# Second node stage of a four-layer graph network: three steps in one flow of seven chunks, with blocks taken two at a time in the halves of the array

## The chip, the cores and the metric

The kernel runs on one core of one Trainium2 chip. The metric is device time in microseconds (us); the time before is 21814.87 us, the median of three runs (21812.7 to 21848.82). The core has a matrix engine (TensorE, called PE in the profile, with its weight loads as PEld), three engines that work on rows of data (VectorE or DVE, ScalarE or ACT, GpSimd or POOL) and SyncE (SP), which issues DMAs here. Engines run side by side and wait for each other by semaphores. TensorE writes to PSUM, and VectorE and ScalarE copy from there to SBUF, from which DMAs go to memory. [...]

## The reference, cut to what matters

Four graph layers run one after the other on 12500 nodes with 64 features and 400000 edges. The stage that is changed closes the second layer and opens the third:

```python
Z = jax.ops.segment_sum(Y, id_Xe[1], num_segments=H.shape[0])      # acc: sums over edges
U_in = jnp.concatenate([H, Z], axis=1)
H_next = jax.nn.relu(U_in @ U_W.T + U_b)
...
x = x + _L1_gnn_ref(h, ...)                                        # x += H_next
h = jnp.maximum(_layernorm(x, axis=-1), 0.0)
# third layer: h @ weight[r] for each of 16 relations r; edges then gather rows of this table
msg = msg + h_src * mask[:, None].astype(feat.dtype) @ weight[r]
```

So for each of the nodes: an update from the old h and the sums, a layer norm, and a row of 16 x 64 = 1024 table values. All is float32.

## The kernel before, in words

The nodes stand in 98 blocks of 128 (`NB`), a block of rows on the 128 partitions, 64 features each. `CH` = 14 blocks make one of seven chunks (`CHUNKS`), `SUB` = 7 blocks one of fourteen half chunks (`SUBS`). The kernel is a row of stages with a barrier after each: building records, gather g0, message_table, gather g1, **update_table** (the stage changed), gather g2, and the last layer. Gather g2 reads the whole table that update_table writes, so nothing of it starts before.

update_table has two parts, one behind the other on TensorE. In the **first part** it takes each half chunk through `turn` (line 1011: h of 7 blocks is transposed by a product with the identity, 128 rows by 64 columns of the array, into `ps_t`), ScalarE copies the result to `ct` (line 971), and `product` (lines 1019 and 1020) adds two products for each block in `ps_u`: the sums `acc` with `uwa`, which takes all 128 rows of the array, and the turned h with `uwh`, which takes 64. VectorE adds bias and relu to x (lines 928 and 931) and runs the layer norm of a chunk (946, 949, 952, 959, 961), with ScalarE's square and square root (992, 998) between. There is one `ps_t`, so the next `turn` waits for ScalarE's copy. ScalarE's order is written out by hand: turned(2k+2), then the square of chunk k, which waits for line 952 of that chunk, then turned(2k+3), then the square root.

In the **second part** `turn_h` (line 1028) transposes the new h, ScalarE copies it (977), and `table_block` (line 1038) makes the 1024 values of a block in two products of 512 columns, with 64 of the array's rows. ScalarE copies the left half of each block (982) and VectorE the right half (936) from one of two `ps_m` to one of two `tb`, and SP writes the block (line 917, 512 KB). Each buffer comes free when its copies or its DMA are done.

A float32 product is two records in the trace, each a pass with a weight load of its own; "x14" for `turn` of 7 blocks is 14 passes.

Of the kernel before, what the change touches and what calls it, by code (L numbers as in the profile page):

```python
# [124 lines left out]
def build(nc, a, out):  # L125
    ctx = ExitStack()
    with ctx:
# [44 lines left out]
        update_table(nc, sem, a, Buffers(arena, b.at), psum, ident, epsc, x, acc, h, table)  # L172
# [711 lines left out]
def update_table(nc, sem, a, b, psum, ident, epsc, x, acc, h, dest):  # L884
# [9 lines left out]
    ct = [b.take(SUB * P) for _ in range(2)]  # L894
    pos = [b.take(SUB * D) for _ in range(2)]
    tb = [b.take(width) for _ in range(2)]
    assert b.at <= ARENA - NB * D
    names = ("w", "t", "ct", "u", "pos", "x", "total", "mid", "sq", "var", "std", "rs", "h", "th", "ht", "mm")
    s_w, s_t, s_ct, s_u, s_pos, s_x, s_total, s_mid, s_sq, s_var, s_std, s_rs, s_h, s_th, s_ht, s_mm = (sem("t2_" + n) for n in names)
    s_ca, s_cv, s_out = ([sem(f"t2_{n}{k}") for k in range(2)] for n in ("ca", "cv", "out"))  # L900
    ps_t = psum[:, 0:SUB * P]
    ps_u = [psum[:, 1024 + 512 * k:1024 + 512 * k + SUB * D] for k in range(2)]
    ps_m = [psum[:, 2048 + 1024 * k:3072 + 1024 * k] for k in range(2)]
    bias = ub.rearrange("p (o f) -> p o f", o=1).to_broadcast([P, SUB, D])

    with nc.Block() as block:
        @block.sync
        def _(sp):
            for k in range(2):
                sp.dma_start(uwa[k * D:(k + 1) * D, :], a["uw"][0:D, :]).then_inc(s_w, 16)  # L910
            sp.dma_start(uwh[0:D, :], a["uw"][D:2 * D, :]).then_inc(s_w, 16)
            sp.dma_start(ub, a["ub"].to_broadcast([P, D])).then_inc(s_w, 16)
            sp.dma_start(w[0:D, :], a["w2"]).then_inc(s_w, 16)
            for n in range(NB):
                sp.wait_ge(s_ca[n % 2], n // 2 + 1)
                sp.wait_ge(s_cv[n % 2], n // 2 + 1)
                sp.dma_start(dest[n * P:(n + 1) * P, :], tb[n % 2]).then_inc(s_out[n % 2], 16)
            for k in range(2):
                sp.wait_ge(s_out[k], 16 * (NB // 2))

        @block.vector
        def _(dve):
            v = nc.vector

            def update(s):
                dve.wait_ge(s_u, s + 1)
# [6 lines left out]
            def take_product(n):  # L933
                dve.wait_ge(s_mm, n + 1)
                wait_earlier(dve, s_out[n % 2], n // 2 * 16)
                v.tensor_copy(tb[n % 2][:, half:], ps_m[n % 2][:, half:]).then_inc(s_cv[n % 2], 1)

            dve.wait_ge(s_w, 80)
# [24 lines left out]
            for n in range(NB):  # L963
                take_product(n)

        @block.scalar
        def _(act):
            def turned(s):
                act.wait_ge(s_t, s + 1)
                wait_earlier(act, s_u, s - 1)  # L970
                nc.scalar.copy(ct[s % 2][0:D, :], ps_t[0:D, :]).then_inc(s_ct, 1)

            def turned_h(s):
                act.wait_ge(s_th, s + 1)

                wait_earlier(act, s_mm, (s - 1) * SUB)
                nc.scalar.copy(ct[s % 2][0:D, :], ps_t[0:D, :]).then_inc(s_ht, 1)

            def take_product(n):
                act.wait_ge(s_mm, n + 1)  # L980
                wait_earlier(act, s_out[n % 2], n // 2 * 16)
                nc.scalar.copy(tb[n % 2][:, 0:half], ps_m[n % 2][:, 0:half]).then_inc(s_ca[n % 2], 1)
# [3 lines left out]
            for k in range(CHUNKS + 1):  # L986
                if k + 1 < CHUNKS:
                    turned(2 * k + 2)
# [4 lines left out]
                if k + 1 < CHUNKS:  # L993
                    turned(2 * k + 3)
                if k >= 1:
# [3 lines left out]
            turned_h(0)  # L999
            for n in range(NB):  # L1000
                if n % SUB == SUB - 2 and n // SUB + 1 < SUBS:
                    turned_h(n // SUB + 1)
                take_product(n)

        @block.tensor
        def _(pe):
            def turn(s):
                wait_earlier(pe, s_ct, s)
                for j in range(SUB):
                    n = s * SUB + j  # L1010
                    last = nc.tensor.matmul(ps_t[0:D, j * P:(j + 1) * P], h[:, n * D:(n + 1) * D], ident, start=True, stop=True)
                last.then_inc(s_t, 1)

            def product(s):
# [761 lines left out]
```

## Time and profile before

| | us |
|---|---|
| median of three runs | 21814.87 |
| the profiled execution | 21835.44 |
| its span, first to last instruction | 21833.6 |
| TensorE busy in the span | 11628.7 (53%) |
| VectorE busy | 11929.5 (55%) |
| GpSimd busy | 15717.8 (72%) |
| mean granted TensorE clock, of 2.4 GHz | 0.667 |

A page of the profile gives each engine's busy time, a row of 40 slices of the span, DMA queues, and the costliest groups of instructions. The stage in question lies at 12403 to 12813 us, less than one slice of 546 us. So the page shows little of it, and what is read below comes from windows, groups by line and the order of instructions in that stretch.

### The profile page before, as it was taken

Reading aid. Unit: us, or ns where it says so; the run is one execution under the profiler, and the core shown is the slowest. Engines: PE = TensorE matmul, PEld = TensorE weight load, DVE = VectorE, ACT = ScalarE, POOL = GpSimd, SP = SyncE. Lnnn points to the kernel's source line nnn. Section 1 sums busy time; section 2 is a strip of 40 time slices with the busy share of each in tenths; the row PEclk is TensorE's granted clock in tenths of the full one; section 3 lists DMA queues with packets and bytes.
Section 4 is the critical chain, followed back from the end, with each engine's and each line's share of the span. In section 5 each row is a group of like instructions: output and inputs, shape, how many; then the busy total and the mean of one; then the engine's idle time right before and its main releaser. Section 6 shows DMA issues by size and latency. Waiting matters only on the chain. (4 is left out here: it accounts for less than half of the span.)

```text
span 21833.6 us, 187489 instructions
## 1 busy us (share of the span) xinstructions
PE 11628.7 (53%) x37787; PEld 5774.8 (26%) x37788; DVE 11929.5 (55%) x22486; ACT 4352.1 (20%) x10620; POOL 15717.8 (72%) x16724
## 2 busy tenths in 40 slices
PE   3777776455555556555555675555555222222246
PEld 1333333222222223222222332222222222222246
DVE  8777777655555555666666545555555222222246
ACT  3000000022222221111111110000000544444456
POOL 3777777777777775777777537777775777777776
PEclk7555555577777777777777777777776555555578
DMA  3333332222222221222222132222221333333366
GB/s 114 98 99 98 98 99 80 72 64 61 63 63 61 63 61 52 63 61 63 61 63 63 38 132 63 61 63 63 61 63 51 111 110 112 110 112 110 112 209 231
DMA packets 997084, 1873.16 MB, mean 86 GB/s; under 512 B 337172, under 2 KB 445620, under 8 KB 983812
## 3 DMA queue, kind: packets, MB, share of 16 engines
q1 hardware_dynamic: 481668, 1217.65, 17.3%
q0 software_dynamic: 506528, 652.41, 12.0%
q10 hardware_dynamic: 8800, 2.08, 0.0%
q8 instruction: 35, 0.57, 0.0%
q14 instruction: 53, 0.43, 0.0%
HBM read 1367.60 MB, written 503.37 MB: 86 GB/s over the span
## 5 line engine op out<-in xcount | busy, mean ns | idle before, releaser
L1289 PE MATMUL psum<-arena 128*128 128x512 f32 x9528 | 6683.6, 865 | 5301.0 <-DMA arena<-table,arena 1824.1
L1162 POOL DMA_INDIRECT arena<-table,arena x6352 | 6002.9, 945 | 2393.0 <-issue 1934.5
L1206 DVE TENSOR_TENSOR arena<-arena,psum 64x256 f32 x9528 | 3997.3, 420 | 4609.2 <-PE psum L1289 2610.5
L1289 PEld LDWEIGHTS psum<-arena 128*128 128x128 f32 x9528 | 2556.9, 283 | 9364.0 <-issue 7078.3
L712 POOL DMA_INDIRECT rec<-arena x3125 | 3003.9, 961 | 1270.4 <-issue 948.9
L1365 POOL DMA_INDIRECT rec<-arena x3176 | 3052.5, 961 | 1095.9 <-issue 962.7
L1162 POOL DMA_INDIRECT arena<-ptable,arena x3176 | 3001.2, 945 | 1115.9 <-issue 967.7
L1180 DVE TENSOR_TENSOR arena<-psum,arena 128x2048 f32<-128x2048 f32 x1191 | 2729.3, 2292 | 37.0
L1453 PE MATMUL psum<-arena 128*128 x6352 | 1086.9, 365 | 2937.4 <-DVE arena L1396 2747.9
L489 PE MATMUL psum<-arena 128*128 128x196 bf16 (+1 forms) x4375 | 1377.9, 428 | 1265.8 <-DVE arena L620 1265.8
L1386 DVE TENSOR_TENSOR arena<-arena 128x136 f32<-128x136 f32 x397 | 119.7, 301 | 2998.1 <-DMA arena<-rec 2997.9
L1453 PEld LDWEIGHTS psum<-arena 128*128 128x128 bf16 x6352 | 842.3, 133 | 3181.8 <-issue 3083.3
L1245 ACT ACTIVATE arena<-arena 128x64 f32<-128x64 f32 x3176 | 801.4, 335 | 3203.5 <-DMA arena<-table,arena 3203.5
L1418 ACT ACTIVATE arena<-arena 128x1024 bf16<-128x1024 bf16 x794 | 866.8, 1139 | 2156.2 <-DMA arena<-lanes 2156.2
L620 DVE TENSOR_TENSOR arena<-psum,arena 128x392 f32<-128x392 f32 x1875 | 918.1, 490 | 361.9 <-PE psum L489 236.6
L1239 ACT ACTIVATE arena<-arena 128x512 f32<-128x512 f32 x397 | 250.2, 630 | 3529.3 <-DVE arena L1186 3529.3
L489 PEld LDWEIGHTS psum<-arena 128*128 128x128 bf16 x4375 | 366.6, 115 | 2191.2 <-DVE arena L620 1815.8
L1423 ACT ACTIVATE arena<-arena 128x1024 bf16<-128x1024 bf16 x794 | 861.9, 1132 | 0.0
L1077 ACT ACTIVATE arena<-arena 128x98 f32<-128x98 f32 x1 | 0.4, 376 | 4060.9 <-DVE arena L734 4060.9
L581 ACT COPY arena<-arena 128x10 f32 (+1 forms) x625 | 127.2, 204 | 3178.1 <-DMA rec<-arena 3072.0
L625 DVE TENSOR_REDUCE arena<-arena 128x10 f32<-128x980 f32 x625 | 734.1, 1175 | 21.6
L1531 POOL TENSOR_SCALAR arena<-arena 128x128 bf16<-128x128 bf16 x880 | 636.5, 740 | 141.2 <-ACT arena L1543 140.1
(218 smaller groups left out, 10728.1 us busy)
## 6 DMA issues: line engine op xcount, KB each, us to landing
arena<-rec SPq DMA_DIRECT2D x297, 1408.0 KB
arena<-rec SPq DMA_DIRECT2D x440, 488.0 KB, 5.7
arena<-in_edge SPq DMA_DIRECT2D x625, 232.0 KB, 2.6
arena<-rec SPq DMA_DIRECT2D x400, 352.0 KB, 3.4
arena<-table,arena POOLq DMA_INDIRECT x6352, 2.5
arena<-lanes SPq DMA_DIRECT2D x99, 1024.0 KB
rec<-arena POOLq DMA_INDIRECT x6301, 2.3
table<-arena SPq DMA_DIRECT2D x196, 512.0 KB, 3.5
```

The lines of the kernel that those rows point to most:

```text
L489: return nc.tensor.matmul(to, identb, one_hots, start=False, stop=False, skip_group_check=True)
L620: v.tensor_tensor(prod[g][:, 2 * n * WIDE:2 * n * WIDE + w], run[:, 0:w], buf[g][:, 2 * n * WIDE:2 * n * WIDE + w], ALU.mult).then_inc(s_s ...
L712: nc.gpsimd.indirect_dma_start(rec, bass.IndirectOffsetOnAxis(ap=stage[g][:, j:j + 1], axis=0), recs[g][:, j * RW:(j + 1) * RW], None).the ...
L1162: nc.gpsimd.indirect_dma_start(rows[q][:, j * D:(j + 1) * D], None, tab, bass.IndirectOffsetOnAxis(ap=idx[:, j, field:field + 1], axis=0)) ...
L1180: v.tensor_tensor(hot[q % HB].rearrange("p (j w) -> p j w", w=LANES), iotas, fields(q, R_DSTL, 1).to_broadcast([P, G, LANES]), ALU.is_equa ...
L1206: v.tensor_tensor(block_sum, block_sum, ps[j // 2][half, j % 2 * LANES:(j % 2 + 1) * LANES], ALU.add).then_inc(s_add[j], 1)
L1245: last = nc.scalar.mul(rows[q][:, at], rows[q][:, at], fields(q, R_W, 1)[:, j, :])
L1289: last = nc.tensor.matmul(ps[u], rows[q][:, 2 * u * D:(2 * u + 2) * D], hot[q % HB][:, u * PAIR:(u + 1) * PAIR], start=True, stop=True)
L1365: nc.gpsimd.indirect_dma_start(slots, bass.IndirectOffsetOnAxis(ap=goal[q][:, j:j + 1], axis=0), rows[q][:, j * ROW:(j + 1) * ROW], None). ...
L1418: nc.scalar.activation(far[q % 2 * WIDEN + k], line, ACT.Square, bias=npid[k]).then_inc(s_far, 1)
L1423: nc.scalar.activation(hot_t[q % HB][:, k * G * P:(k + 1) * G * P], far[q % 2 * WIDEN + k], ACT.Relu, bias=ones[:, 0:1], scale=-1.0).then_ ...
L1453: last = nc.tensor.matmul(ps_m[q % 2][:, j * 256:j * 256 + HW], hot_t[q % HB][:, (k * G + j) * P:(k * G + j + 1) * P], hparts[:, bass.ds(a ...
```

## The change

Only `update_table` changes, and its call, which now also passes `shared`, a stretch of SBUF that this stage did not use.

- Both parts become one loop over k of `CHUNKS + 3` = 10 steps. In step k TensorE does: the updates of chunk k+1, the turning of old h for chunk k+2, the first 7 of 14 table units of chunk k-3 (`EARLY`), the turning of new h for chunk k-2, and the other 7 units. VectorE and ScalarE have their copies of table units spread between the steps of update and norm.
- Blocks are taken two at a time, block j of the first half chunk and block j of the second (`side` 0 and 1). Turning puts them on partitions 0 to 63 and 64 to 127 of one `ps_t`, so the copy of `ct` or `ht` is 128 x 896 for a whole chunk in place of two of 64 x 896. The products with `uwh` and with `w` use rows 0 to 63 of the array for one block and rows 64 to 127 for the other; `uwh` and `w` are loaded twice for that, one load for each half of the partitions.
- A table unit `u` is 512 columns of two blocks. ScalarE copies side 0 and VectorE side 1, so each makes 98 copies of 128 x 512, as before. There are still two sets of PSUM (`DUO` = 2), now of 1024 words as two banks, one for each side, and four `tb` of one block each, in place of two.
- In the updates the two products with `acc` come first and then the two with `ct`, in place of one of each by turns.
- `ct` and `ht` are now separate buffers, two of each.

```diff
-    ct = [b.take(SUB * P) for _ in range(2)]
+    ct, ht = ([b.take(SUB * P) for _ in range(2)] for _ in range(2))
...
-    tb = [b.take(width) for _ in range(2)]
...
+    extra = Buffers(shared)
+    tb = [extra.take(width) for _ in range(4)]
...
-    ps_m = [psum[:, 2048 + 1024 * k:3072 + 1024 * k] for k in range(2)]
+    DUO = 2
+    ps_m = [[psum[:, 2048 + 1024 * u + 512 * k:2048 + 1024 * u + 512 * (k + 1)] for k in range(2)] for u in range(DUO)]
+    PAIRS_K = NB // 2
+    EARLY = SUB
+    LAGS = CHUNKS + 3
     bias = ub.rearrange("p (o f) -> p o f", o=1).to_broadcast([P, SUB, D])
+    sides = [slice(k * D, (k + 1) * D) for k in range(2)]
...
             for k in range(2):
...
+                sp.dma_start(uwa[sides[k], :], a["uw"][0:D, :]).then_inc(s_w, 16)
+                sp.dma_start(uwh[sides[k], :], a["uw"][D:2 * D, :]).then_inc(s_w, 16)
+                sp.dma_start(w[sides[k], :], a["w2"]).then_inc(s_w, 16)
             sp.dma_start(ub, a["ub"].to_broadcast([P, D])).then_inc(s_w, 16)
...
+            for t in range(PAIRS_K):
+                for k, taken in ((0, s_ca), (1, s_cv)):
+                    n = t // SUB * CH + k * SUB + t % SUB
+                    sp.wait_ge(taken, 2 * t + 2)
+                    sp.dma_start(dest[n * P:(n + 1) * P, :], tb[t % 2 * 2 + k]).then_inc(s_out[t % 2 * 2 + k], 16)
+            for k in range(4):
+                sp.wait_ge(s_out[k], 16 * (-(-(PAIRS_K - k // 2) // 2)))
...
+            def take_products(k, units):
+                if not 0 <= k < CHUNKS:
+                    return
+                for u in range(k * CH + units[0], k * CH + units[1]):
+                    t, c = u // 2, u % 2 * half
+                    dve.wait_ge(s_mm[1], u + 1)
+                    if c == 0:
+                        wait_earlier(dve, s_out[t % 2 * 2 + 1], t // 2 * 16)
+                    v.tensor_copy(tb[t % 2 * 2 + 1][:, c:c + half], ps_m[u % DUO][1]).then_inc(s_cv, 1)
+            dve.wait_ge(s_w, 112)
             update(0)
             update(1)
-            for k in range(CHUNKS + 2):
+            for k in range(LAGS):
                 if k + 1 < CHUNKS:
                     update(2 * k + 2)
+                take_products(k - 3, (0, 2))
                 if k < CHUNKS:
                     dve.wait_ge(s_x, 2 * k + 2)
...
+                take_products(k - 3, (2, 4))
                 if 0 <= k - 1 < CHUNKS:
...
+                take_products(k - 3, (4, 6))
                 if k < CHUNKS:
...
+                take_products(k - 3, (6, EARLY))
                 if k + 1 < CHUNKS:
                     update(2 * k + 3)
-                if 0 <= k - 2:
+                if 0 <= k - 2 < CHUNKS:
...
+                take_products(k - 3, (EARLY, CH))
...
         @block.scalar
         def _(act):
...
+            def turned(k):
+                act.wait_ge(s_t, k + 1)
+                wait_earlier(act, s_u, k - 1)
+                nc.scalar.copy(ct[k % 2], ps_t).then_inc(s_ct, 1)
+            def turned_h(k):
+                act.wait_ge(s_th, k + 1)
+                for side in range(2):
+                    wait_earlier(act, s_mm[side], (k - 1) * CH)
+                nc.scalar.copy(ht[k % 2], ps_t).then_inc(s_ht, 1)
+            def take_products(k, units):
+                if not 0 <= k < CHUNKS:
+                    return
+                for u in range(k * CH + units[0], k * CH + units[1]):
+                    t, c = u // 2, u % 2 * half
+                    act.wait_ge(s_mm[0], u + 1)
+                    if c == 0:
+                        wait_earlier(act, s_out[t % 2 * 2], t // 2 * 16)
+                    nc.scalar.copy(tb[t % 2 * 2][:, c:c + half], ps_m[u % DUO][0]).then_inc(s_ca, 1)
             turned(0)
             turned(1)
...
+            for k in range(LAGS):
+                if k + 2 < CHUNKS:
+                    turned(k + 2)
+                take_products(k - 3, (0, EARLY - 1))
                 if k < CHUNKS:
...
+                take_products(k - 3, (EARLY - 1, EARLY))
+                if 0 <= k - 1 < CHUNKS:
...
+                if 0 <= k - 2 < CHUNKS:
+                    turned_h(k - 2)
+                take_products(k - 3, (EARLY, CH))
...
         @block.tensor
         def _(pe):
...
+            def turn(k, semaphore):
                 for j in range(SUB):
...
+                    for side in range(2):
+                        n = k * CH + side * SUB + j
+                        last = nc.tensor.matmul(ps_t[sides[side], j * P:(j + 1) * P], h[:, n * D:(n + 1) * D], ident, start=True, stop=True)
+                last.then_inc(semaphore, 1)
+            def turn_old(k):
+                wait_earlier(pe, s_ct, k)
+                wait_earlier(pe, s_ht, k - 4)
+                turn(k, s_t)
+            def turn_new(k):
+                pe.wait_ge(s_h, k + 1)
+                wait_earlier(pe, s_ht, k)
+                pe.wait_ge(s_ct, min(k + 5, CHUNKS))
+                turn(k, s_th)
+            def updates(k):
+                pe.wait_ge(s_ct, k + 1)
+                wait_earlier(pe, s_pos, 2 * k)
                 for j in range(SUB):
...
+                    to = [ps_u[side][:, j * D:(j + 1) * D] for side in range(2)]
+                    for side in range(2):
+                        n = k * CH + side * SUB + j
+                        nc.tensor.matmul(to[side], acc[:, n * P:(n + 1) * P], uwa, start=True, stop=False)
+                    for side in range(2):
+                        last = nc.tensor.matmul(to[side], ct[k % 2][sides[side], j * P:(j + 1) * P], uwh[sides[side], :], start=False, stop=True)
                 last.then_inc(s_u, 1)
...
+            def table_units(k, units):
+                if not 0 <= k < CHUNKS:
+                    return
+                for u in range(k * CH + units[0], k * CH + units[1]):
+                    j, c = u % CH // 2, u % 2 * half
+                    if u % CH == 0:
+                        pe.wait_ge(s_ht, k + 1)
+                    wait_earlier(pe, s_ca, u - DUO + 1)
+                    wait_earlier(pe, s_cv, u - DUO + 1)
+                    for side in range(2):
+                        nc.tensor.matmul(ps_m[u % DUO][side], ht[k % 2][sides[side], j * P:(j + 1) * P], w[sides[side], c:c + half],
+                                         start=True, stop=True).then_inc(s_mm[side], 1)
+            pe.wait_ge(s_w, 112)
+            turn_old(0)
+            turn_old(1)
+            updates(0)
+            for k in range(LAGS):
+                if k + 1 < CHUNKS:
+                    updates(k + 1)
+                if k + 2 < CHUNKS:
+                    turn_old(k + 2)
+                table_units(k - 3, (0, EARLY))
+                if 0 <= k - 2 < CHUNKS:
+                    turn_new(k - 2)
+                table_units(k - 3, (EARLY, CH))
```

## Rows read from the trace of the kernel before

**Rows 1.** Windows of the stage: start and end, length, busy of each engine, clock, DMA share, GB/s.
```profile
12410.00:12500.00 90.00, 76.65 (x308) 64.15 (x308) 13.19 (x18) 8.18 (x10) 0.00 (x0) 0.58 0.00 1
12500.00:12596.00 96.00, 72.12 (x279) 59.92 (x279) 23.81 (x32) 10.49 (x15) 0.00 (x0) 0.55 0.00 0
12606.00:12640.00 34.00, 34.00 (x73) 15.54 (x73) 8.58 (x12) 7.35 (x12) 0.00 (x0) 0.69 0.42 168
12640.00:12812.00 172.00, 170.17 (x503) 79.16 (x501) 60.13 (x87) 60.84 (x99) 0.00 (x0) 1.00 0.65 263
```

**Rows 2.** Groups by line: busy us, mean ns of one, idle before and releaser.
```profile
L1011 PE MATMUL psum<-arena 128*64 128x128 f32 x196 | 45.5, 425 | 42.6 <-ACT arena L971 30.8 <-DMA arena<-in_w 11.8
L1019 PE MATMUL psum<-arena 128*128 128x64 f32 x196 | 59.1, 398 | 6.1 <-ACT arena L971 6.1
L936 DVE COPY arena<-psum 128x512 f32<-128x512 f32 x98 | 67.7, 691 | 137.0 <-DMA table<-arena 74.4 <-PE psum L1038 62.5
L982 ACT COPY arena<-psum 128x512 f32<-128x512 f32 x98 | 57.4, 586 | 129.0 <-DMA table<-arena 79.1 <-PE psum L1038 49.8
L971 ACT COPY arena<-psum 64x896 f32<-64x896 f32 x14 | 12.5, 892 | 57.1 <-PE psum L1011 57.1
L928 DVE TENSOR_TENSOR arena<-psum,arena 128x448 f32<-128x448 f32 x14 | 8.7, 625 | 156.2 <-PE psum L1020 156.2
L961 DVE SCALAR_TENSOR_TENSOR arena<-arena 128x896 f32<-128x896 f32 x7 | 7.7, 1093 | 0.2
L959 DVE RECIPROCAL arena<-arena 128x14 f32<-128x14 f32 x7 | 1.6, 232 | 0.0
```

**Rows 3.** Timeline of TensorE, first part: start, length, instructions, idle before.
```profile
12410.31 3.25 PE L1011 MATMUL psum<-arena 128*64 128x128 f32 x14 [11.80 <-DMA arena<-in_w]
12414.54 3.25 PE L1011 MATMUL psum<-arena 128*64 128x128 f32 x14 [0.99 <-ACT arena L971]
...
12465.57 0.69 PE L1019 MATMUL psum<-arena 128*128 128x64 f32 x2
12466.19 0.61 PE L1020 MATMUL psum<-arena 64*128 64x64 f32 x2
12466.73 0.43 PE L1019 MATMUL psum<-arena 128*128 128x64 f32 x2
12467.09 0.43 PE L1020 MATMUL psum<-arena 64*128 64x64 f32 x2
...
12470.61 0.69 PE L1019 MATMUL psum<-arena 128*128 128x64 f32 x2
12478.05 1.33 PE L1011 MATMUL psum<-arena 128*64 128x128 f32 x5 [6.13 <-ACT arena L971]
```

**Rows 4.** Timeline of TensorE, second part.
```profile
12605.61 17.43 PE L1038 MATMUL psum<-arena 64*128 64x512 f32 x20 [5.87 <-ACT arena L977]
12622.97 3.25 PE L1028 MATMUL psum<-arena 128*64 128x128 f32 x14
12626.14 12.69 PE L1038 MATMUL psum<-arena 64*128 64x512 f32 x28
12638.77 1.74 PE L1028 MATMUL psum<-arena 128*64 128x128 f32 x14
```

**Rows 5.** Timeline, other stages: runs of passes of one shape at either clock.
```profile
16802.54 42.05 PE L1071 MATMUL psum<-arena 128*128 128x64 f32 x196 [3.34 <-PEq L110]
8378.46 3.25 PE L861 MATMUL psum<-arena 64*128 64x64 f32 x14
8384.57 1.77 PE L861 MATMUL psum<-arena 64*128 64x64 f32 x14
```

**Rows 6.** Line 917, the table's DMAs, and its row in the page's list of issues.
```profile
L917 SPq DMA_DIRECT2D table<-arena x98: 332/332/355, 12610.2 to 12811.7; - x98
table<-arena SPq DMA_DIRECT2D x196, 512.0 KB, 3.5
```

**Rows 7.** Windows of the loads that open gather g2, columns as in group 1.
```profile
12821.00:12823.00 2.00, 0.00 (x0) 0.00 (x0) 2.00 (x1) 0.00 (x0) 0.70 (x1) 0.50 1.04 400
```

**Rows 8.** Timeline of SP at the stage's start.
```profile
12403.86 1.12 SPq L910 DMA_DIRECT2D arena<-in_uw  x2
12406.29 0.47 SPq L913 DMA_DIRECT2D arena<-in_w  x1
```

More of the change, by code:

```diff
@@ L171, in build @@
         sem.end_stage()
-        update_table(nc, sem, a, Buffers(arena, b.at), psum, ident, epsc, x, acc, h, table)
+        update_table(nc, sem, a, Buffers(arena, b.at), psum, ident, epsc, x, acc, h, shared, table)
         sem.end_stage()
@@ L881, in _, with update_table @@
                 product(s)
-def update_table(nc, sem, a, b, psum, ident, epsc, x, acc, h, dest):
+def update_table(nc, sem, a, b, psum, ident, epsc, x, acc, h, shared, dest):
     width = R * D
@@ L925, in update @@
             def update(s):
-                dve.wait_ge(s_u, s + 1)
+                dve.wait_ge(s_u, s // 2 + 1)
                 wait_earlier(dve, s_x, s - 1)
@@ L998, in _ @@
                     nc.scalar.activation(rs[:, at], var[:, at], ACT.Sqrt, bias=epsc, scale=1.0 / D).then_inc(s_std, 1)
[L999 to L1003, printed above, removed]
+                if 0 <= k - 2 < CHUNKS:
+                    turned_h(k - 2)
+                take_products(k - 3, (EARLY, CH))
         @block.tensor
         def _(pe):
-            def turn(s):
-                wait_earlier(pe, s_ct, s)
+            def turn(k, semaphore):
@@ L1009, in turn @@
                 for j in range(SUB):
[L1010 to L1014, printed above, removed]
-                pe.wait_ge(s_ct, s + 1)
-                wait_earlier(pe, s_pos, s - 1)
-                for j in range(SUB):
-                    n = s * SUB + j
-                    nc.tensor.matmul(ps_u[s % 2][:, j * D:(j + 1) * D], acc[:, n * P:(n + 1) * P], uwa, start=True, stop=False)
-                    last = nc.tensor.matmul(ps_u[s % 2][:, j * D:(j + 1) * D], ct[s % 2][0:D, j * P:(j + 1) * P], uwh[0:D, :], start=False, stop=True)
-                last.then_inc(s_u, 1)
@@ L1023, in turn_h @@
-            def turn_h(s):
-                pe.wait_ge(s_h, s // 2 + 1)
-                wait_earlier(pe, s_ht, s)
-                for j in range(SUB):
-                    n = s * SUB + j
-                    last = nc.tensor.matmul(ps_t[0:D, j * P:(j + 1) * P], h[:, n * D:(n + 1) * D], ident, start=True, stop=True)
-                last.then_inc(s_th, 1)
-            def table_block(n):
-                s, j = n // SUB, n % SUB
-                if j == 0:
-                    pe.wait_ge(s_ht, s + 1)
-                wait_earlier(pe, s_ca[n % 2], n // 2)
-                wait_earlier(pe, s_cv[n % 2], n // 2)
-                for c in (0, half):
-                    last = nc.tensor.matmul(ps_m[n % 2][:, c:c + half], ct[s % 2][0:D, j * P:(j + 1) * P], w[0:D, c:c + half],
-                                            start=True, stop=True)
-                last.then_inc(s_mm, 1)
@@ L1042, in _ @@
-            pe.wait_ge(s_w, 80)
-            turn(0)
-            for s in range(SUBS):
-                if s + 1 < SUBS:
-                    turn(s + 1)
-                product(s)
-            pe.wait_ge(s_ct, SUBS)
-            turn_h(0)
-            for n in range(NB):
-                table_block(n)
-                if n % SUB == SUB - 3 and n // SUB + 1 < SUBS:
-                    turn_h(n // SUB + 1)
+                    for side in range(2):
+                        n = k * CH + side * SUB + j
+                        last = nc.tensor.matmul(ps_t[sides[side], j * P:(j + 1) * P], h[:, n * D:(n + 1) * D], ident, start=True, stop=True)
```

41 lines of the change are left out of this document (4 added, 37 removed).

## The prediction

> **What bounds the stage now.** The stage runs on its own between two barriers, so what it gains or loses is what the kernel gains or loses. I read the windows first [rows 1]: in the first part, 12410 to 12597 us, TensorE is busy 76.65 of 90 and 72.12 of 96 us, and no other engine is above a quarter. In the second, 12606 to 12812, it is busy 34 of 34 and 170.17 of 172 us. So TensorE's order sets the stage, and the question is at which clock its passes run and what makes it wait.
>
> The clock is read from the spacing of the passes. In the first part two passes take 0.62 us at 1.2 GHz (12465.57 to 12466.19) and 0.36 at 2.4 GHz (12466.73 to 12467.09), and the fast spell is short [rows 3]; the granted clock of 0.58 and 0.55 says the same [rows 1]. In the second part 28 passes of 512 columns take 12.69 us, mostly 0.43 each, once TensorE has worked without a gap for some 20 us; the 20 passes before took 17.43, most of them 0.86 [rows 4]. After that the clock is 1.00 throughout [rows 1].
>
> The waits: in the first part the turning idles 30.8 us and the product 6.1 us for the copy of line 971 [rows 2], mostly in gaps of 5 to 6 us a chunk (6.13 before 12478.05), and about 1 us where only the copy is late [rows 3]. The long gaps come from ScalarE's written order: turned(2k+3) stands behind the square, which waits for VectorE's line 952, which waits for products of TensorE. In the second part 524 KB at 263 GB/s are 1.99 us a block [rows 1], 0.25 of it the seventh part of a turning (1.74 [rows 4]), so **1.74 us** for the block itself. Lines 936 and 982 wait for DMAs 74 to 79 us and for TensorE 50 to 63 us [rows 2]: the two are about equally late there. The stage runs from the first pass at 12410.31 [rows 3] to the last table DMA at 12811.7 [rows 6]: **401.4 us**.
>
> **The change, part by part.** Prices are at 1.2 and 2.4 GHz.
>
> *Turning.* 14 passes take 3.25 or 1.74 us [rows 3, 4], so a chunk of 28 takes 6.5 or 3.5. Now consecutive products write to different halves of the array's columns. No row shows two such products; the bounds are no overlap (6.5 / 3.5) and full overlap (3.25 / 1.75). A turning pass loads 64 columns of weights and streams 128; a pass the other way round, 128 loaded and 64 streamed, takes 0.2145 us (42.05 / 196 [rows 5]), so the load of 64 needs no more than half of the 0.23. It is the streaming that two halves could share, and I take full overlap, and keep the other end.
>
> *Updates.* Passes of one shape in a row cost 0.2145 to 0.232 us at the lower clock and 0.126 at the higher [rows 5], but by turns between 128 rows and 64 rows of the array they cost 0.31 and 0.18 [rows 3]. So each change of shape costs about 0.17 / 0.12. A pair of blocks had 4 changes and 8 passes (2.48 / 1.45 us) and has 2 changes and 8 passes now: 8 x 0.22 + 2 x 0.17 = 2.1, or 8 x 0.122 + 2 x 0.12 = 1.22. Seven pairs: 15.1 / 8.5 us a chunk, before 17.4 / 10.2. Overlap of the two products with `ct` is not counted: the weight load of 128 columns is what spaces these passes.
>
> *Table.* A unit is two products, 4 passes: 1.71 / 0.86 us if the halves of the rows work at once, 3.42 / 1.72 if not. No row shows the overlap. The group's name says that each pass uses 64 of 128 rows [rows 4], and if the products start in order, the first pass of side 1 can still run beside the second of side 0. I take full overlap; the other end is a rival. A copy then becomes the limit: with two PSUM sets a set is refilled after 3 passes (1.29), a copy of 0.691 us [rows 2] and some 0.25 of handing over, so 2.24 for two units, **1.12 us** a unit at the higher clock, and (2.57 + 0.94) / 2 = **1.8** at the lower. The four `tb` add a DMA limit: a block's DMA lands 3.5 us after its issue [rows 6]; with 0.69 + 0.69 of copies behind it, two pairs of buffers turn in 5.6 us, 1.4 a unit once the first four of a run have used up the slack. The DMA engines allow more: 263 GB/s took a share of 0.65 [rows 1], loads ran at 400 GB/s [rows 7], so 524 KB need no less than 1.31 us. Seven units in a run: 4 x 1.12 + 3 x 1.5 = 9 us at the higher clock, 12.6 at the lower.
>
> [...]
>
> *Waits.* The gaps of 5 to 6 us go: ScalarE now copies `ct` before it waits for line 952. What is late next: about 1.1 us for the copy (0.99 in [rows 3]) four times in the opening, where nothing stands between a turning and its update. New is TensorE's wait for h in `turn_new`, in the middle of the units. Behind it stand units 7 to 13, and so both copiers and the DMAs. The wait is from the end of unit 6: copy 0.8, update 1.25 (twice line 928's 0.625), reciprocal 0.23, line 961's 1.09 [rows 2] and hand-overs, 3.7 us; from chunk 3 of the table on no update is left, 2.3. In the opening, turn_new(0) waits for a whole round of VectorE after updates(3), 7.4 us, of which turn_old(4) covers 3.25: 4.1.
>
> *Loads.* Two more DMAs on SP, 0.6 us each (1.12 for two [rows 8]): 1.2 us later at the start.
>
> *Clock.* The flow mixes stretches that had the lower clock (updates) with dense 512-column work that had the higher. I expect the lower clock in updates, as in the first part of before, and about half of each in the units and new turnings, as waits and updates come between them: the first seven units of a chunk near the lower price while updates stand before them, 10.5 to 11 else.
>
> **The sum**, at the lower clock for updates:
> - Opening, up to updates(4): 4 updates of 15.1, 6 turnings of 3.25, waits 3.3 + 4.1 = 87; the short fast spells of the first part take 7 off: 80.
> - Steps 3 and 4: 15.1 + 3.25 + 12.6 + 3.7 + 3.0 + 11, less 1 for a fast spell, = 48 each; step 5 has no old turning, 45: 141.
> - Steps 6 to 8: 10.5 + 2.3 + 2.5 + 10.5 = 26 each: 78. Step 9: 21.
> - Start 1.2 and end 1.
>
> Together 322, so 401 - 322 = **79 us less**. On the profiled execution of 21835.4 that gives 21756; that execution lies 20.6 above the median, to which the forecast applies: 21814.9 - 79 = **21736**. The forecast's own range: at the lower clock throughout 354 us (21768), without overlap of the turnings another 20 to 30 (up to 21790); with the higher clock in all units, 9 us for each seven, 288 (21702).
>
> **Rivals.**
> - *The higher clock holds throughout.* For: the second part held it for 170 us [rows 1]. [...] Opening 53, steps 3 to 5 99, 6 to 8 66, step 9 20, ends 2: 240 us, so 21654.
> - *The halves do not work at once.* Then the change does less than it says; a unit is 3.42 / 1.72 us. [...] TensorE is dense in the units, so the clock rises late in each early run: opening 100, steps 3 to 5 179, 6 to 8 90, step 9 24, ends 2 = 395 us, so 21809, no change.
> - *Slower: serial halves at the lower clock.* If besides the wait for h, every step, drops the clock to 1.2 GHz and updates hold it there, seven units cost 24 us. Opening 100, steps 3 and 4 80 each, step 5 73, steps 6 to 8 57 each, step 9 48, ends 2: 554 us, so 21967. It decides once the units run below 2.4 GHz for over about half their time without overlap, a stage of over 445 us. Against: such dense work brought the clock up within about 20 us before [rows 4].
>
> **Chances.** Forecast 0.60, higher clock 0.12, serial halves 0.22, slower 0.06. A difference of 0.2% (44 us) is about what a measurement of this kernel can tell from no change. Of the forecast's share a tenth lies within 44 us, of the serial case's a little on either side: faster 0.68, same 0.25, slower 0.07. The range leaves out the slower rival and half of the fastest: 21670 to 21820.
>
> **What would show it.** In the profile of after: the stage's length, 322 us from first pass to last table DMA. Start times of the table's passes: side 0 and side 1 side by side, a unit every 1.1 to 1.8 us; if the passes of a unit never overlap, the halves are serial. Turning of a chunk in 3.3 us at the lower clock against 6.5. Updates of a chunk near 15 us. TensorE's idle before the turning of new h, 2 to 4 us, released by line 961's successor. No gap of 5 us for `ct`. Spacing in the table's passes of 0.43 or 0.86 gives the clock. The prediction is wrong if the halves are serial, if the updates run at 2.4 GHz, or if DMAs of four buffers land later than 3.5 us so that units cost 1.75 us throughout.

## The result, and the profile after

| | us |
|---|---|
| before, median of 5 runs beside it | 21828.78 (21812.7 to 21848.82) |
| after, median of 5 runs | 21683.96 (21672.23 to 21689.39) |
| ratio | 0.9936, interval 0.9926 to 0.9947 |
| span of the profiled execution, before and after | 21833.6 and 21670.0 |
| the stage, first pass to last table DMA, before and after | 401.4 and 274.9 |

The kernel is 145 us faster. The forecast was 79 us, 21736; the range of 21670 to 21820 holds the time. Of the 145 us the stage gives 126. In the two profiled executions the stage also begins 15 us earlier, and what follows it is 22 us shorter, in stages that the change does not touch; I come back to that.

The windows of the stage after (columns as in [rows 1]) are the opening, steps 3, 4 and 5, and the rest:

```profile
12395.00:12465.00 70.00, 59.59 (x394) 51.88 (x395) 18.94 (x26) 7.99 (x11) 0.00 (x0) 0.60 0.00 1
12465.00:12505.00 40.00, 33.00 (x168) 20.87 (x167) 14.56 (x21) 11.00 (x18) 0.00 (x0) 0.72 0.34 138
12505.00:12540.00 35.00, 27.96 (x171) 16.77 (x169) 16.10 (x24) 11.12 (x20) 0.00 (x0) 0.85 0.53 214
12540.00:12573.00 33.00, 24.91 (x134) 14.47 (x136) 15.42 (x23) 9.56 (x16) 0.00 (x0) 0.79 0.50 202
12573.00:12671.00 98.00, 68.71 (x316) 30.34 (x315) 45.93 (x69) 37.77 (x64) 0.00 (x0) 0.93 0.78 316
```

TensorE is no longer busy throughout: 68.71 of the last 98 us. The clock is 0.60 in the opening and 0.93 in the last window, with 0.85 in step 4 and 0.79 in step 5 between. The lower and the higher clock, which the prediction calls 1.2 and 2.4 GHz, are granted clocks of 0.50 (12443.5 to 12446.2) and 1.00 (12573 to 12585); the windows give these shares and no frequency. The DMAs move 316 GB/s in the last window, against 263 in [rows 1]. That is a mean over units and turnings. In a run of units with no turning in it the DMA engines are full:

```profile
12573.00:12585.00 12.00, 8.91 (x36) 3.22 (x35) 8.47 (x13) 5.08 (x9) 0.00 (x0) 1.00 1.01 404
```

At 404 GB/s the 524 KB that a unit makes take 1.30 us, an estimate from this row.

The timeline of TensorE after shows each term of the sum (start, length, instructions, idle before). First the opening, then a chunk of units:

```profile
12395.21 3.25 PE L1031 MATMUL psum<-arena 128*64 128x128 f32 x28 [12.34 <-DMA arena<-in_ub]
...
12443.84 0.69 PE L1054 MATMUL psum<-arena 64*128 64x64 f32 x4
12444.46 1.11 PE L1052 MATMUL psum<-arena 128*128 128x64 f32 x4
12445.50 0.69 PE L1054 MATMUL psum<-arena 64*128 64x64 f32 x4
12446.13 1.11 PE L1052 MATMUL psum<-arena 128*128 128x64 f32 x4
...
12461.38 3.25 PE L1031 MATMUL psum<-arena 128*64 128x128 f32 x28 [4.10 <-DVE arena L978]
...
12492.48 3.26 PE L1031 MATMUL psum<-arena 128*64 128x128 f32 x28 [3.75 <-DVE arena L978]
...
12572.83 1.99 PE L1067 MATMUL psum<-arena 64*128 64x512 f32 x8 [1.56 <-DVE arena L949]
12575.39 1.99 PE L1067 MATMUL psum<-arena 64*128 64x512 f32 x8 [0.57 <-DVE arena L949]
12577.94 1.99 PE L1067 MATMUL psum<-arena 64*128 64x512 f32 x8 [0.57 <-DVE arena L949]
...
12586.98 3.11 PE L1031 MATMUL psum<-arena 128*64 128x128 f32 x28 [2.73 <-DVE arena L978]
```

Three things are to be seen. The halves work at once: 28 passes of turning take 3.25 us, as 14 did [rows 3], and 8 passes of 512 columns take 1.99 us, where one after the other at 0.43 each [rows 4] would need 3.4, an estimate. Two units come every 2.56 us, 1.28 each, about what the full DMA engines allow. TensorE waits 0.57 us of it for VectorE's copy (line 949), and the first copy of each such pair had itself waited for a DMA of the table (1.27 us before 12574.55 and before 12577.11). And the wait for the new h (line 978, the old 961) stands before each turning of new h.

### The profile page after: what moved, and what is told of

Read it like the earlier page. It is cut to its first block and busy times, and to the rows that moved or that the text cites. A ratio compares the mean times of both kernels' runs of the same rounds, so it can differ in the third digit from the quotient of the medians.

```text
span 21670.0 us, 187257 instructions
## 1 busy us (share of the span) xinstructions
PE 11478.3 (53%) x37787; PEld 5677.5 (26%) x37788; DVE 11916.9 (55%) x22486; ACT 4346.3 (20%) x10606; POOL 15688.8 (72%) x16724
## 5 line engine op out<-in xcount | busy, mean ns | idle before, releaser
L1318 PE MATMUL psum<-arena 128*128 128x512 f32 x9528 | 6680.8, 864 | 5287.7 <-DMA arena<-table,arena 1819.9
```

Source lines behind the costliest of these rows:

```text
L1318: last = nc.tensor.matmul(ps[u], rows[q][:, 2 * u * D:(2 * u + 2) * D], hot[q % HB][:, u * PAIR:(u + 1) * PAIR], start=True, stop=True)
```

## The experiments

On two of the chips used here every kernel, the one before too, takes 26.4 to 26.8 thousand us. The time is added in other stages: in the profile of after_again the products of line 1318 are preceded by 8308.1 us of idle, in that of after by 5287.7, with nearly the same busy time. The changed stage keeps its length there, 278.4 us for the kernel after against 274.9. So I compare stages, from the first pass to the issue of the last table DMA, and give medians against the kernel before on the same chip. The stage before was profiled on one chip only.

| kernel | stage, us | median less that of before, us |
|---|---|---|
| before | 401.4 | |
| order_only | 381.7 | -7 (one run) |
| flow_only | 360.5 | -45 |
| halves_only | 271.4 | -131 |
| after | 274.9 | -145 |
| after_again | 278.4 | -109 |
| h_first | 238.9 | -163 |
| h_first_eight | 222.3 | -171 (one run) |
| interleaved | 217.3 | -180 |
| ct_serial | 295.5 | -107 (one run) |
| turn_serial | 294.2 | -104 (one run) |
| table_serial | 423.0 | -8 (one run) |
| table_serial_again | 411.4 | +19 (one run) |

With eight buffers (h_first_eight and interleaved, below) more is still under way when the last DMA is issued: the next stage issues its first DMA 4.6 us later in after and h_first, 7.3 in h_first_eight and 7.1 in interleaved.

### Halves without the flow, and the flow without halves

**halves_only** puts the table behind the last update, with blocks still in pairs:

```diff
-    LAGS = CHUNKS + 3
+    LAGS = CHUNKS + 9
...
-                table_units(k - 3, (0, EARLY))
-                if 0 <= k - 2 < CHUNKS:
-                    turn_new(k - 2)
-                table_units(k - 3, (EARLY, CH))
+                table_units(k - 9, (0, EARLY))
+                if 0 <= k - 8 < CHUNKS:
+                    turn_new(k - 8)
+                table_units(k - 9, (EARLY, CH))
```

with the same shift for ScalarE's and VectorE's copies and for turned_h. The turning of new h now waits until all of `ct` is copied.

> The blocks still go two at a time in the halves of the array, but the table waits for the last update: two parts one behind the other, as before. Stage after the change: 275 us from first pass to last table DMA. Theory A (the halves are the gain, the one flow brings nothing, since TensorE works through its order one by one either way and the flow adds a wait for the new h in each chunk): updates and turnings 7 x (11.7 + 3.3) + 8 of waits = 113, gap for h 8, table 7 x (1.75 + 14 x 1.28) = 138, together about 258 us, so at or below the kernel after the change, ratio to before about 0.993. Rival B (the flow brings a third or more of the gain, by keeping TensorE busy while copies and DMAs run): 310 us or more, ratio 0.996.

Measured: stage 271.4 us, ratio 0.9951 (0.9935 to 0.9968). It has ScalarE's new order too (see order_only). Theory A holds: **the flow adds nothing to the halves**. The table's part of its timeline:

```profile
15814.89 7.84 PE L1066 MATMUL psum<-arena 64*128 64x512 f32 x24 [10.05 <-ACT arena L994]
15824.31 1.13 PE L1066 MATMUL psum<-arena 64*128 64x512 f32 x4 [1.59 <-DVE arena L949]
15825.37 1.75 PE L1031 MATMUL psum<-arena 128*64 128x128 f32 x28
15827.05 5.18 PE L1066 MATMUL psum<-arena 64*128 64x512 f32 x20
```

There is one gap of 10.05 us between the parts, and then no wait for h in front of any turning: it takes 1.75 us at a granted clock of 1.00 (15825.4 to 15827.1) right behind a unit. What the flow saves at the seam and in the updates (75.2 us of products against 83.8 here) it pays back in seven waits for h, 25.0 us.

**flow_only** keeps the flow and lets both blocks use the same rows or columns (it does not compute the values of the side 1 blocks):

```diff
-   matmul(ps_t[sides[side], ...
+   matmul(ps_t[sides[0], ...
-   ct[k % 2][sides[side], ...], uwh[sides[side], :]
+   ct[k % 2][sides[0], ...], uwh[sides[0], :]
-   ht[k % 2][sides[side], ...], w[sides[side], c:c + half]
+   ht[k % 2][sides[0], ...], w[sides[0], c:c + half]
```

> One flow as after the change, but all products of side 1 use the same rows or columns of the array as side 0, so no two can run at once (the values of the side 1 blocks are wrong for it; the work in instructions and bytes is the same). Theory A (the halves are the whole gain): turnings 14 x 3.2 = 45 us more, the products with the turned h 7 x 4 = 28, table units 1.8 to 2 in place of 1.3 at the higher clock and twice at the lower, 50 to 60: stage 395 us or more, ratio to before about 1.000. Rival B (the flow alone gives a third or more): stage 350 us or less, ratio 0.998.

Measured: stage 360.5 us, ratio 0.9983 (0.9973 to 0.9993). This lies between the two expectations: everything but the halves brings 41 us. That is not the flow by itself, since the kernel also has ScalarE's new order, the grouping of the updates' products by shape, and four `tb`. The updates' products sum to 92.2 us here (45.3 and 46.9), against 118.0 in the kernel before (59.1 in [rows 2] and 58.9 in the row below), and ScalarE's order is worth 20 us in the next experiment. No run has the flow without these, so a gain of its own is not shown.

```profile
L1020 PE MATMUL psum<-arena 64*128 64x64 f32 x196 | 58.9, 395 | 0.0
```

The group of its table passes, and that of after (the second row):

```profile
L1067 PE MATMUL psum<-arena 64*128 64x512 f32 x392 | 182.5, 625 | 0.0
```
```profile
L1067 PE MATMUL psum<-arena 64*128 64x512 f32 x392 | 104.1, 645 | 28.5 <-DVE arena L949 23.0 <-ACT arena L1004 4.8
```

The same 392 passes keep TensorE for 182.5 us instead of 104.1, and it waits for no copy.

### ScalarE's order alone

**order_only** is the kernel before with one line of ScalarE's order moved:

```diff
                 if k + 1 < CHUNKS:
                     turned(2 * k + 2)
+                    turned(2 * k + 3)
                 if k < CHUNKS:
...
-                if k + 1 < CHUNKS:
-                    turned(2 * k + 3)
```

> The kernel before with one line moved: ScalarE copies turned(2k+3) before the square of chunk k and not after it. Theory A (the long gaps of TensorE in the first part came from ScalarE's order): the gaps of 5 to 6 us a chunk go, 37 us of idle fall to about 10, and with TensorE dense the clock may rise: stage 401 less 25 to 45, 355 to 375 us, which is the whole of what the flow without the halves gains (41 us). Rival B (the gaps come from the single ps_t buffer, and what is moved changes nothing): 395 us or more.

Measured: 381.7 us, 20 less than before. The size falls short of theory A's 25 to 45, and the timeline shows that the gaps went all the same. The turning's group and the second part:

```profile
L1010 PE MATMUL psum<-arena 128*64 128x128 f32 x196 | 44.9, 421 | 12.0 <-DMA arena<-in_w 11.0 <-ACT arena L971 1.0
```
```profile
15685.82 17.43 PE L1037 MATMUL psum<-arena 64*128 64x512 f32 x20 [6.09 <-ACT arena L977]
...
15762.34 7.13 PE L1037 MATMUL psum<-arena 64*128 64x512 f32 x16
15770.78 9.86 PE L1037 MATMUL psum<-arena 64*128 64x512 f32 x12 [1.30 <-DVE arena L936]
15780.57 3.25 PE L1027 MATMUL psum<-arena 128*64 128x128 f32 x14
```

The idle for ScalarE's copy falls from 36.9 us [rows 2] to 1.0, and the first part from 195.3 us (12410.31 to 12605.61, [rows 3, 4]) to 154.2: **41 us**, 36 of it gaps and most of the rest updates at a slightly higher clock (granted 0.61 in the first part, 0.57 before). Then the second part takes 227.5 us against 206.1: behind one wait of 1.30 us, from 15769.5 on, passes go from 0.43 to 0.82 us and the turning from 1.74 to 3.25 (granted clock 0.51 from 15771 to 15809, 1.00 before). With that the second part takes 21 us back. So in the first part this one line, which needs no flow, brings as much as flow_only in all, and 20 us are left of it in this one run. All kernels with the new code have it.

### Each pair of halves alone

**ct_serial**, **turn_serial** and **table_serial** make one of the three edits of flow_only each.

> Only the products of the turned old h (64 of 128 rows) use rows 0 to 63 for both blocks (x of the side 1 blocks is wrong for it). In the profile of after the four passes of a pair take 0.62 us at the lower clock and 0.37 at the higher. The prediction held that the weight load spaces these passes, so that the halves give nothing here (Theory A: stage within 3 us of the 275 to 278 after). Rival B: weight loads in the two halves of the rows overlap too, and without the halves the four passes take 1.0 us and 0.55: 49 x 0.3 = 15 to 20 us longer.

Measured: 295.5 us, 17 to 21 more than after: rival B. The group of the turned products without the halves and, second, in after:

```profile
L1054 PE MATMUL psum<-arena 64*128 64x64 f32 x196 | 47.4, 384 | 0.0
```
```profile
L1054 PE MATMUL psum<-arena 64*128 64x64 f32 x196 | 29.6, 393 | 0.0
```

The timeline of a pair of blocks at the lower clock (granted 0.50 from 12442 to 12445):

```profile
12442.09 1.11 PE L1052 MATMUL psum<-arena 128*128 128x64 f32 x4
12443.14 1.11 PE L1054 MATMUL psum<-arena 64*128 64x64 f32 x4
12444.18 1.11 PE L1052 MATMUL psum<-arena 128*128 128x64 f32 x4
```

Without the halves the four passes of line 1054 take 1.04 us from start to start, with them 0.62 (12443.84 to 12444.46 above). The loads of line 1054 take 0.27 us each in both kernels, and together they cover 38.9 us in ct_serial and 21.2 in after. So the weight loads in the two halves of the rows run beside each other too.

> Only the turning writes to PSUM partitions 0 to 63 for both blocks (the blocks of side 1 are wrong for it). Theory A (consecutive turnings in different halves of the columns overlap fully): a turning of 28 passes goes from 3.25 to 6.5 us at the lower clock and from 1.75 to 3.4 at the higher; 14 of them with about a third at the higher clock, 35 to 40 us longer, about 312 us, unless TensorE's longer activity raises the clock and gives 10 to 20 back. Rival B (only the rows matter): within 5 us of 275 to 278.

Measured: 294.2 us, 16 to 19 more. The turnings keep TensorE 72.6 us against 42.7, 30 more, near theory A's 35 to 40. 11 to 14 came back: the waits for h are 20.6 us against 25.0, the table's passes sum to 101.4 us against 104.1, and the updates' products to 70.7 against 75.2, at a slightly higher clock (granted 0.81 over the stage against 0.79).

> Only the table's products of side 1 use rows 0 to 63, like side 0 (the table rows of the side 1 blocks are wrong for it). Theory A (the halves work at once, and the copies bound a unit at 1.28 us): a unit takes 4 x 0.43 = 1.72 us and some 0.1 at the higher clock, so 98 x 0.5 = 50 us longer at least, stage 325 to 345 us. Rival B (the halves hardly overlap, the gain is from elsewhere): stage below 290 us.

Measured: **423.0 us**, 150 more than after and 22 more than before. Neither theory: the overlap is real, but its loss costs three times the 50 us expected, since 252 of the 392 passes took 0.86 us, the spacing at a granted clock of 0.50 (15918 to 15966), and 140 took 0.44 or 0.45. Here are runs of both kinds in table_serial, and below flow_only, which has more serial work:

```profile
15765.22 24.26 PE L1067 MATMUL psum<-arena 64*128 64x512 f32 x28
...
15804.26 12.65 PE L1067 MATMUL psum<-arena 64*128 64x512 f32 x28
...
15889.70 24.61 PE L1067 MATMUL psum<-arena 64*128 64x512 f32 x56
15918.35 48.15 PE L1067 MATMUL psum<-arena 64*128 64x512 f32 x56
15971.74 24.55 PE L1067 MATMUL psum<-arena 64*128 64x512 f32 x56
16000.38 72.05 PE L1067 MATMUL psum<-arena 64*128 64x512 f32 x84
```
```profile
15830.58 12.28 PE L1067 MATMUL psum<-arena 64*128 64x512 f32 x28
15936.26 24.30 PE L1067 MATMUL psum<-arena 64*128 64x512 f32 x56
16029.53 36.31 PE L1067 MATMUL psum<-arena 64*128 64x512 f32 x84
```

For the last 84 passes in a row a pass takes 0.86 us in the one (granted clock 0.50) and 0.43 in the other (1.00). In flow_only only 28 of the 392 passes, at 15903.18, took 0.86.

> The kernel of table_serial once more: its stage took 423 us, with the units of 28 passes at 24.3 us (lower clock), while flow_only, with more serial work, took 360 us with 12.3 us (higher clock). Theory A (which clock the units get depends on the order of waits and dense work, so on the kernel): 24 us for the first units and 415 to 430 us again. Rival B (it is a matter of the moment at which the run begins, and falls otherwise each time): the stage comes out elsewhere between 330 and 430 us.

Measured on another chip: 411.4 us. The last runs alternate as before (24.52, 48.15, 24.46 and 72.05 us); of the early ones two of 28 passes took 12.4, where one did, so 224 passes ran at the lower clock, 0.86 us each. That speaks for theory A, that most of the lower clock belongs to that kernel, though the length just misses the window expected for it. What in the kernel decides it stays open.

### Where the wait for h goes, and what is late next

**h_first** moves the block that makes h(k-2) on VectorE (wait for s_std, reciprocal, scalar_tensor_tensor) ahead of `update(2 * k + 2)`, with nothing else changed.

> The reciprocal and the scaling that make the new h of chunk k-2 are moved to the head of VectorE's step, before the updates and copies. After the change TensorE waits 38 us before the turning of new h and loads, 25 of them for the step that makes h (2.6 to 5.1 us each). Theory A: nothing else is late there, all seven waits go and the stage gets 20 to 25 us shorter, about 252 us. Rival B: the copies of the units, moved back by 1.3 us, or the DMAs of the table come to be late next, and the gain is below 10 us.

Measured: 238.9 us, ratio 0.9945 (0.9928 to 0.9962); 36 to 40 less than after and after_again. All seven waits are gone; the group of the turning in h_first:

```profile
L1031 PE MATMUL psum<-arena 128*64 128x128 f32 x392 | 35.8, 356 | 13.5 <-DMA arena<-in_ub 11.4 <-ACT arena L987 2.1
```

and after:

```profile
L1031 PE MATMUL psum<-arena 128*64 128x128 f32 x392 | 42.7, 405 | 38.3 <-DVE arena L978 25.0 <-DMA arena<-in_ub 12.3 <-ACT arena L987 1.0
```

25.0 us of waiting went, and with it another 11 to 15, of which 7 are turnings at a higher clock (35.8 against 42.7 us for the same passes) and 4 to 5 are updates (70.7 against 75.2). The granted clock over the stage is 0.84, and 0.79 in after.

**h_first_eight** has eight `tb` besides, four pairs in turn (`tb[t % 4 * 2 + k]`).

> h_first with eight tb in place of four. Theory A (copies bound the units, the waits of VectorE for DMAs of the table, 45 us in h_first, are mostly hidden by TensorE's wait for copies): 0 to 8 us less than 239. Rival B (the DMAs of four buffers bound the units): 20 us less or more, 1.15 us a unit.

Measured: 222.3 us, 17 less: nearer to B. Up to the next stage's first DMA it is 14 less (229.6 against 243.6). VectorE's waits for the table's DMAs fall from 44.9 to 16.9 us (h_first, then h_first_eight):

```profile
L949 DVE COPY arena<-psum 128x512 f32<-128x512 f32 x98 | 64.3, 688 | 65.5 <-DMA table<-arena 44.9 <-PE psum L1067 20.6
```
```profile
L949 DVE COPY arena<-psum 128x512 f32<-128x512 f32 x98 | 65.8, 688 | 42.8 <-PE psum L1067 26.0 <-DMA table<-arena 16.9
```

So in after the four buffers, and with them the landing of DMAs, held back the copies that TensorE seemed to wait for. With eight, nine units in a row take 1.02 us each, with no wait shown:

```profile
15688.83 9.21 PE L1067 MATMUL psum<-arena 64*128 64x512 f32 x36
```

The DMAs now go on through turnings and updates, and the engines stay full over whole steps. The first window is h_first_eight, the second interleaved, which comes next:

```profile
15680.00:15720.00 40.00, 36.46 (x188) 14.14 (x186) 28.82 (x42) 22.14 (x39) 0.00 (x0) 1.00 1.02 405
15660.00:15700.00 40.00, 37.72 (x192) 14.05 (x190) 25.97 (x39) 21.47 (x38) 0.00 (x0) 1.00 1.02 405
```

**interleaved** goes further: eight `tb`, h one step earlier, and on TensorE a piece of other work behind each unit:

```diff
+            NEW = {0: (0, 2), 1: (2, 4), 2: (4, 6), 3: (6, 7)}
+            OLD = {11: (0, 3), 12: (3, 5), 13: (5, 7)}
+            for k in range(LAGS):
+                for i in range(CH):
+                    table_units(k - 4, (i, i + 1))
+                    if i in NEW:
+                        turn_new(k - 3, NEW[i])
+                    elif i in OLD:
+                        turn_old(k + 2, OLD[i])
+                    else:
+                        updates(k + 1, (i - 4, i - 3))
```

> The flow of the changed kernel, but each unit of the table is followed by one piece of an update or of a turning (an update of one pair of blocks takes 0.96 us at the higher clock), the new h is made a step earlier, and there are eight tb. Theory A (TensorE stands idle in each unit for the copy, some 0.57 us in 2.57 for two units, and the copiers and DMAs stand idle during updates, so only interleaving makes the one flow pay): opening four steps of 15 = 60, seven steps of 14 x 1.45 = 142, together 205 us. Rival B (TensorE's order is the bound, pieces and units add up as before): 235 us or more, no better than h_first at 239.

Measured: 217.3 us, ratio 0.9926 (0.9908 to 0.9944), median 26409.21 us (26394.19 to 26410.96) beside 26480.3 us (26471.89 to 26490.99) for the kernel after on the same chip (after_again). It beats both kernels, by 71 us over after. But only 5 us of that is the interleaving, since h_first_eight has 222.3. Theory A's 205 was not reached, and the theory had no term for the DMA engines: 98 blocks of 524 KB at 405 GB/s are 127 us, an estimate from the windows above, and the first is issued 82.5 us after the first pass. Together that is 209 us to the landing of the last, and some 5 less to its issue. So 205 would have needed full engines from the first DMA on, and what is left to gain in such a kernel lies mostly in the opening.

> The kernel after the change itself, beside the others of this call, as the reference for stage lengths on the same chip. The stage had 275 us from first pass to last table DMA. If a stage length is a property of the kernel, it is 270 to 280 again; if the clock falls otherwise from run to run, it can be off by 20 us or more, and the comparisons of single profiles are worth no more than that.

Measured: 278.4 us, as expected. A stage length repeats within some 4 us for this kernel and within 12 for table_serial, by two profiles each; so the 5 us of interleaved over h_first_eight, and the 3 to 7 of halves_only under after, are not told from zero by single profiles.

## Why the prediction was right, and where it was off

The forecast was right in direction and in its main mechanism, the overlap of the halves, and short by 66 us in size, 47 of them in the stage: 322 predicted, 274.9 measured. That is nearer to the 240 of its first rival, the higher clock throughout. Two terms are off. The updates are seven chunks at 15.1, 106 us, less some 10 for fast spells, and their products took 75.2 (45.6 and 29.6); without the overlap they took 93.9 (ct_serial, 46.5 and 47.4), so nearly all of this error is the overlap that was not counted. The units add up to 155 us in the sum, and the table's passes with the waits for copies took 132.6 (104.1 and 28.5), since the clock was above the "about half of each" of the text.

- **Opening**, 80 predicted, 69.4 measured (12395.21 to 12464.56). The term for updates failed: "Overlap of the two products with `ct` is not counted: the weight load of 128 columns is what spaces these passes." A chunk takes 7 x 1.67 = 11.7 us at the lower clock, not 15.1, and ct_serial shows why. The price of grouping by shape was right: without the overlap a pair takes 2.09 us there, as summed (2.1). The wait for the first h was 4.10 (4.1 predicted); the others in the opening were 1.00 for ScalarE's copy and 5.1 for VectorE, where the sum had 3.3.
- **Turnings**: full overlap, 3.25 us for 28 passes, as taken. That a load of 64 columns needs no more than half of the 0.23, the reason given for it, is not shown: in the kernel before, the records of the loads last 0.226 us in line 1011 (64 columns) and 0.269 in line 1019 (128).
- **Steps 3 and 4**, 48 predicted each, 40.7 and 34.7 measured (12464.56 to 12505.25 to 12539.92). In step 3 the updates give 3.4 us, the units, quicker than the price at the lower clock, most of the rest. In step 4 most of the updates ran at the higher clock, a pair in 0.96 us (granted clock 1.00 from 12505 to 12508); "the lower clock in updates" was wrong for most of steps 4 and 5. The prediction named updates at the higher clock as a sign that it is wrong, and for these two chunks that sign came.
- **Units**: 1.12 us if copies bound them, 1.5 when DMAs do; measured about 1.04 for the first five of a run (5.18 us for 20 passes) and 1.28 after. Once no updates are left seven take 9.1 to 10.3 us, near the 9 us of the price at the higher clock (the sum has 10.5), but by two errors that cancel: copies allow 1.02 (h_first_eight), and the DMAs bind at 1.28, by the full engines. The prediction had that bound, "no less than 1.31 us", and set it aside for one from the landing time. Of that one the terms named, 3.5 and twice 0.69, make 4.9 us and not 5.6, and 3.5 is a median over the 196 DMAs of two stages [rows 6]. The 0.25 us of handing over in the price of 1.12 is shown by no run; 1.02 leaves 0.06 for it (2.04 for two units less 1.29 and 0.69), an estimate.
- **Wait for h**: 3.7 predicted beside updates and 2.3 after them; measured 3.75, 3.94 and 5.13, then 2.73, 2.64 and 2.71. Right in place and nearly in size. But its price is not its length alone: without it the stage is 36 us shorter, not 25, in part by the clock.
- **Step 5 to the end**, 144 predicted, 130 measured (12539.92 to 12670.1), from the updates of step 5 and the clock: the last window stands at 0.93, above the half and half of the sum.
- **The gaps of 5 to 6 us** came from ScalarE's order, as the text had it: order_only leaves 1.0 of 36.9 us [rows 2]. What is late next in the changed kernel is ScalarE's copy once (1.00 us; the text says four times 1.1, its sum has three) and, once the updates follow each other, VectorE's bias add that frees `ps_u`, 5.1 us in all in the opening. The two more DMAs cost less than the 1.2 us predicted: the idle before the first pass is 12.34 us against 11.80 [rows 3], and it lies ahead of the stage as measured here.
- **Outside the stage**: 19 us of the 145 are not in it. Where the same comparison was made on other chips, medians and stages moved alike (halves_only -131 and -130, h_first -163 and -162.5, flow_only -45 and -41) or the median less (after_again -109 and -123). In the single runs the two differ by up to 30 us (order_only -7 and -20, table_serial -8 and +22, table_serial_again +19 and +10). So 19 us are within what differs without a known cause, and they are not shown to be an effect of the change.

Of the rivals, serial halves did not happen (8 passes of 512 columns in 1.99 us), but the slower one was closer than its chance of 0.06 says. Once only the table's products are made serial in this flow, 252 and 224 of the 392 passes take 0.86 us, the lower clock, and the stage is longer than before (423.0 and 411.4 us). Its threshold was put at 445 us, the 401.4 of before and 44 more; the two runs stay under that. The reason I gave against it, that dense work brings the clock up within some 20 us [rows 4], did not hold there.

The copies by themselves are only a small part of TensorE's wait here. With eight buffers a unit takes 1.02 us, against 0.86 for its four passes of 0.43, two at a time; the rest of the wait is the DMAs'.

## What to carry to other kernels

Pairing products that use half of the array's rows or columns paid here in float32, and for short passes too (four of 64 columns in 0.62 us instead of 1.04). With ScalarE's order, products grouped by shape and four buffers it gave 130 us of a stage of 401, and the one flow gave nothing beside it. Before overlapping stages on an engine that works in written order, ask what it waits for in the middle: moving the step that it waits for ahead of others (h_first) gave 36 us for seven moved lines, more than the flow. When copies look like the limit, see what they wait for, and look at the DMA share in a window of such a run alone: four more buffers took 14 to 17 us off here, and then the DMA engines were full at 405 GB/s.

## What the hardware showed that I had not expected

- Weight loads for the upper and the lower half of the rows overlapped: four passes of 64 columns with 128 columns of weights take 0.62 us in two halves (after) and 1.04 us in one (ct_serial), both at a granted clock of 0.50.
- Dense passes of 512 columns did not always bring the clock up: in table_serial 84 passes in a row took 72.05 us, 0.86 each, at a granted clock of 0.50, with waits of 6.2 us in all in the last 157 us, while in flow_only 84 such passes took 36.31 at 1.00. Both are dense; I have no cause to name.
- The clock fell once behind a short wait. In order_only the passes ran at 0.43 us until a wait of 1.30 us and near 0.82 behind it (granted clock 1.00 from 15763 to 15769, 0.51 from 15771 to 15809). That the wait did it is not shown: in after, waits of 2.13 and 2.36 us (before 12597.33 and 12629.09) left the units behind them at a granted clock of 1.00 (12597 to 12602 and 12629 to 12634). With the waits of 3 to 5 us gone (h_first) the same turnings and updates took 7 and 4 to 5 us less.
- With four or eight buffers the table's DMAs of 512 KB filled the DMA engines at 404 to 405 GB/s (share 1.01 and 1.02); with two buffers they moved 263 GB/s at a share of 0.65 [rows 1].
